# Experts with a bitwise threshold search and down products last, the last norm over two stages, and filler products on TensorE ahead of four stages

## What is computed

```python
aff = jax.nn.sigmoid(flat_x @ gate_w + expert_bias)
_, topk_idx = jax.lax.top_k(aff, TOP_K)
mask = (topk_idx[:, :, None] == jnp.arange(E_r)[None, None, :]).any(axis=1)
score = jnp.where(mask, aff, -1.0).T
_, sel_idx = jax.lax.top_k(score, capacity)          # capacity = 1024 // 7 = 146
kept = jnp.take_along_axis(mask.T, sel_idx, axis=1)
w = jnp.where(kept, jnp.take_along_axis(aff.T, sel_idx, axis=1), 0.0)
out = jax.vmap(_ffn)(flat_x[sel_idx], routed_w1, routed_w2)
routed_sum = jnp.zeros_like(flat_x).at[sel_idx].add(out * w[:, :, None])
return shared_sum + routed_sum                       # x = x + gb * this
```

## Time and profile before

| what | value |
|---|---|
| median of three runs | 858.86 us (857.44 to 860.13) |
| profiled execution | 859.08 us |
| its span | 857.3 us |
| mean granted TensorE clock | 0.934 of full |
| busy PE, PEld, DVE, ACT, POOL | 727.9, 630.3, 615.7, 478.8, 376.4 us |
| norm ahead of the experts | 740.0 to 754.5 us |
| experts | 754.5 to 857.3 us |

### The profile page before, as it was taken

How to read it: one execution, slowest core, us unless ns; L and a number is a source line. 1 busy time by engine, 2 the same in 40 slices (tenths; PEclk the granted TensorE clock), 3 DMA queues, 4 the chain that set the end, 5 groups by cost and what they waited for, 6 DMA issues and landing times. The chain is left out here.

```text
span 857.3 us, 13269 instructions
## 1 busy us (share of the span) xinstructions
PE 727.9 (85%) x4368; PEld 630.3 (74%) x4368; DVE 615.7 (72%) x1313; ACT 478.8 (56%) x961; POOL 376.4 (44%) x389
## 2 busy tenths in 40 slices
PE   4769999899998999999999589972889998579980
PEld 2558888788887888878888489972667786548870
DVE  3645776667666776766776798986488878569988
ACT  2445666656675666755665434324587867155761
POOL 1193565515655156550451250002445544037883
PEclk9778999999999999999999989985899999889995
DMA  7340000000000000000000000004000000000001
GB/s 269 108 120 7 13 26 13 14 1 14 25 15 13 0 13 12 13 13 1 7 7 7 1 1 2 1 1 148 1 1 0 1 1 1 1 1 2 1 0 50
DMA packets 19723, 19.77 MB, mean 23 GB/s; under 512 B 1998, under 2 KB 17870, under 8 KB 19662
## 3 DMA queue, kind: packets, MB, share of 16 engines
q1 hardware_dynamic: 18334, 17.84, 6.6%
q10 hardware_dynamic: 1328, 1.18, 0.5%
HBM read 17.97 MB, written 1.05 MB: 22 GB/s over the span
## 5 line engine op out<-in xcount | busy, mean ns | idle before, releaser
L1000 POOL TENSOR_TENSOR at_swapped<-at_swapped,at_sin 128x512 f32<-128x512 f32 x40 | 51.7, 1292 | 180.0 <-ACT at_swapped L781 180.0
L816 ACT ACTIVATE at_probs<-at_probs,at_negmax 128x128 f32<-128x128 f32 (+7 forms) x128 | 99.5, 778 | 27.7 <-DVE at_negmax L895 24.5
L895 DVE CUSTOM_DVE_ANT_0 at_probs<-at_scores,causal 128x128 f32<-128x128 f32 (+7 forms) x128 | 96.4, 753 | 24.1 <-PE at_scores L698 21.9
L709 PE MATMUL at_turn<-ident_sb,at_probs 128*128 128x128 f32 x576 | 86.7, 278 | 12.2 <-DVE at_full_T_lo L910 11.4
L709 PEld LDWEIGHTS at_turn<-ident_sb,at_probs 128*128 128x128 f32 x576 | 67.6, 142 | 20.6 <-issue 6.5
L808 ACT ACTIVATE at_edge_T_hi<-at_turn 128x128 fp32r<-128x128 f32 (+3 forms) x128 | 55.5, 434 | 41.4 <-PE at_turn L709 41.1
L696 PE MATMUL at_scores<-at_kT_hi,room 128*128 128x512 f32 (+1 forms) x192 | 69.2, 360 | 10.6 <-POOL room L1022 5.1
L697 PE MATMUL at_scores<-at_kT_lo,room 128*128 128x512 f32 (+1 forms) x192 | 68.5, 357 | 0.0
L698 PE MATMUL at_scores<-at_kT_hi,room 128*128 128x512 f32 (+1 forms) x192 | 68.2, 355 | 0.0
L808 ACT ACTIVATE at_full_T_hi<-at_turn 128x512 fp32r<-128x512 f32 x64 | 38.3, 599 | 50.1 <-PE at_turn L709 48.3
L910 DVE TENSOR_TENSOR at_edge_T_lo<-at_turn,at_edge_T_hi 128x128 fp32r<-128x128 f32 (+3 forms) x128 | 61.3, 479 | 2.4 <-ACT at_edge_T_hi L808 2.4
(11 more groups left out here) (360 smaller groups left out, 2467.3 us busy)
## 6 DMA issues: line engine op xcount, KB each, us to landing
at_wq_in<-L_attn_Wqkv SPq DMA_DIRECT2D x16, 128.0 KB, 2.2
at_wo_in<-L_attn_Wo SPq DMA_DIRECT2D x16, 128.0 KB, 2.1
staging<-L_ffn_routed_w SPq DMA_DIRECT2D x7, 256.0 KB, 4.2
wmod<-L_wmod SPq DMA_DIRECT2D x3, 512.0 KB, 8.1
wmod<-L_wmod SPq DMA_DIRECT2D x1, 1536.0 KB, 11.4
x<-L_attn_x ACTq DMA_DIRECT2D x1, 1024.0 KB, 6.2
at_wkv_in<-L_attn_Wqkv SPq DMA_DIRECT2D x8, 128.0 KB, 4.7
staging<-L_ffn_w_gate SPq DMA_DIRECT2D x1, 1024.0 KB, 5.3
```

Of the source, the lines that this page charges most:

```text
L709: mm = pe.transpose(p_turn[t % 2][:, b - b0, :], probs[:, s % 4, b * P:(b + 1) * P], m.ident[:, :])
L816: act.activation(row, row, ACT.Exp, scale=-1.0, bias=negmax[:, s % 4:s % 4 + 1], accum_out=rowsum[:, s // NT % 2, i:i + 1])\
L895: dve.tensor_tensor_reduce(out=probs[:, s % 4, 0:width], in0=p_scores[s % 2][:, 0:width], in1=m.causal[:, S - width:], scale=-1.0, scalar= ...
L1000: pool.tensor_tensor(swapped[:, b, :], swapped[:, b, :], sin[:, cols], ALU.mult).then_inc(rope_turned, 1)
```

## The change

`keep_warm` issues matmuls of 128x512 whose output nobody reads: 5 at the end of `opening`, 7 and 9 around the first two transposes of `ffn0`, 50 and 12 around those of `attention1`'s first block, 12 and 12 at the end of its second.

`transposed_rows` is gone. The norm of tiles 0 to 3 goes into the tail of `attention1` (normalised by ScalarE with scale and bias, `spread`), with the variances of tiles 4 to 7; the rest of tiles 4 to 7 goes into `ffn1`.

In `ffn1` the sixteen half-expert slots run first, up products only, and all eight down products behind them, with `fed` kept for every expert. VectorE multiplies straight from PSUM (x1 isn't copied any more). The ranking is replaced by a search for each expert's 146th largest score, bit by bit, three bits a round: VectorE forms eight candidate bounds with a bitwise or, compares all scores with them, TensorE counts by a product with ones (eight matmuls of 64 columns), VectorE keeps the largest bound that at least 146 scores reach; ten rounds, in slots 4 to 13. Ties at the bound are ordered by a product in slot 14 (`find_order`, `weigh`). So the weights are there before the first down product, `y` is gone, and each output is added from PSUM; a bank's next product waits for its readers. GpSimd and ScalarE take tiles 0 and 1 in place of 6 and 7. The semaphores of the norms become shared ones; `steps`, a table of digits, is loaded by SP at `ffn1`'s start.

```diff
...
+def keep_warm(pe, out, w, count):
+    for _ in range(count):
+        pe.matmul(out, w[:, 0:P], w[:, 0:BANK], start=True, stop=True)
...
                 mod_columns(1, 0, 12)
+                keep_warm(pe, p_rows[0][:, :], wmod[:, 0, 0, :], 5)
...
+                idle_bank = p_gate[:, 0:2, :].rearrange("p e t -> p (e t)")
+                keep_warm(pe, idle_bank, m.room, 7)
                 turn_x(0)
                 turn_x(1)
+                keep_warm(pe, idle_bank, m.room, 9)
...
+                    keep_warm(pe, idle_bank[:, :], m.room, 50)
...
+                    keep_warm(pe, idle_bank[:, :], m.room, 12)
...
                     out_job(1, j)
+                keep_warm(pe, p_scores[1][:, BANK:S], m.room, 12)
...
+                keep_warm(pe, p_scores[1][:, BANK:S], m.room, 12)
...
+                load_table(act, m, ACT.Sqrt, 0)
+                variance_roots(act, m, FIRST_TILES, 5)
+                act.wait_ge(spread_ready, 1)
+                for n in FIRST_TILES:
+                    act.activation(ln_xn[:, n, :], m.x[:, n, :], ACT.Identity, scale=m.rstd[:, n:n + 1], bias=m.nbias[:, n:n + 1]).then_inc(ln_normed, 1)
+                for k in range(KD):
+                    act.wait_ge(ln_turned, k + 1)
+                    act.activation(ln_h32[:, k, :], ln_banks[k], ACT.Identity, scale=m.modcol[:, 1, 8 + k:9 + k], bias=m.modcol[:, 1, 6 + k:7 + k])\
+                        .then_inc(ln_scaled, 1)
+                variance_roots(act, m, LAST_TILES, 6)
...
+                def final_stats(tiles):
+                    for n in tiles:
+                        dve.wait_ge(proj_free, len(jobs) + 4 + n // 2 + 1)
+                        chain.step(dve.bn_stats(m.stats[:, n, :], m.x[:, n, :]))
+                chain = m.chain.on(dve)
+                add_out(1, 0)
+                add_out(1, 1)
+                final_stats(FIRST_TILES)
+                add_out(1, 2)
+                variances(dve, m, chain, FIRST_TILES)
+                add_out(1, 3)
+                inverse_roots(dve, m, chain, FIRST_TILES, 5)
+                spread(dve, m, FIRST_TILES).then_inc(spread_ready, 1)
+                final_stats(LAST_TILES)
+                variances(dve, m, chain, LAST_TILES)
+                for k in range(KD):
+                    cols = slice(0, BANK)
+                    dve.wait_ge(ln_scaled, k + 1)
+                    chain.run(dve.tensor_copy(m.hT.hi[:, k, cols], ln_h32[:, k, :]))
+                    dve.tensor_tensor(m.hT.lo[:, k, cols], ln_h32[:, k, :], as_f32(m.hT.hi[:, k, cols]), ALU.subtract)
...
-    transposed_rows(nc, m, sems, sb, 1, 6, "ln3")
     E8 = NE + 1
+    DIGIT, ROUNDS = 8, 10
...
+        by_row, p_aff, p_marked, score, p_kept = (part(2, n * NT * E8) for n in range(5))
+        cut = p_y[2][:, 1, DM - E8:DM]
+        counts, order = part(3, 0), part(3, DM)
...
+        POOL_TILES, OWN_TILES = (0, 1), (2, 3, 4, 5, 6, 7)
+        NP, NO = len(POOL_TILES), len(OWN_TILES)
+        slots = [(0, 0), (1, 0), (0, 1), (1, 1)] + [(e, c) for e in range(2, E8) for c in range(2)]
+        GATED_SLOTS = (0, 1, 2)
+        FIRST_ROUND = 4
+        ORDER_SLOT = FIRST_ROUND + ROUNDS
...
+                def count(r):
+                    pe.wait_ge(compared, r + 1)
+                    out = counts[:, :, :].rearrange("p t e -> p (t e)")
+                    for t in range(NT):
+                        mm = pe.matmul(out, ones[:, :], above[:, t, :, :].rearrange("p j e -> p (j e)"), start=(t == 0), stop=(t == NT - 1))
+                    mm.then_inc(counted, 1)
+                def find_order():
+                    pe.wait_ge(split_done, 2)
+                    pe.matmul(order[:, :, :], earlier[:, :], equal[:, :, :], start=True, stop=False)
+                    for t in range(NT):
+                        pe.matmul(order[:, :, :], ones[:, :], more[:, t:t + 1, :].broadcast_to([P, NT, E8]), start=False, stop=False)
+                    for t in range(NT - 1):
+                        rest = NT - 1 - t
+                        mm = pe.matmul(order[:, t + 1:, :], ones[:, :], equal[:, t:t + 1, :].broadcast_to([P, rest, E8]), start=False, stop=(t == NT - 2))
+                    mm.then_inc(ordered, 1)
...
+                            own = [t for t in OWN_TILES if t // 2 <= j]
+                            pooled = [t for t in POOL_TILES if t // 2 <= j]
+                            if own:
+                                pe.wait_ge(routed_added, NO * (e - 2) + len(own))
+                            if len(pooled) > 2 * j:
+                                pe.wait_ge(scaled_done, NP * (e - 2) + len(pooled))
...
+                find_logits(0)
+                up(0)
+                turn_x()
+                up(1)
+                pe.wait_ge(hT_ready, KD)
+                find_logits(1)
+                up(2)
+                turn_logits()
+                up(3)
+                for n in range(FIRST_ROUND, len(slots)):
+                    up(n)
+                    if n < ORDER_SLOT:
+                        count(n - FIRST_ROUND)
+                    elif n == ORDER_SLOT:
+                        find_order()
+                for e in range(E8):
+                    down(e)
...
+                load_table(act, m, ACT.Silu, 2)
+                feed_hi(2)
+                for n in range(3, len(slots)):
...
+                def middle(n):
+                    dve.wait_ge(x2_read, n + 1)
+                    if n >= 2:
+                        dve.wait_ge(fed_lo, n - 1)
+                    gate = act2[:, n % 2, :]
+                    if n in GATED_SLOTS:
+                        chain.run(dve.tensor_tensor(gate, p_x2[n % 2][:, :], gate, ALU.mult))
+                    dve.tensor_tensor(mid[:, n % 2, :], p_x1[n % 2][:, :], gate, ALU.mult).then_inc(mid_done, 1)
...
+                def compare(r):
+                    as_int = mybir.dt.int32
+                    digits = steps[:, r, :].unsqueeze(2).broadcast_to([P, DIGIT, E8])
+                    chain.run(dve.tensor_tensor(bounds[:, :, :].bitcast(as_int), cut.bitcast(as_int).unsqueeze(1).broadcast_to([P, DIGIT, E8]),
+                                                 digits, ALU.bitwise_or))
+                    dve.tensor_tensor(above[:, :, :, :], score[:, :, :].unsqueeze(2).broadcast_to([P, NT, DIGIT, E8]),
+                                      bounds[:, :, :].unsqueeze(1).broadcast_to([P, NT, DIGIT, E8]), ALU.is_ge).then_inc(compared, 1)
+                def raise_cut(r):
+                    dve.wait_ge(counted, r + 1)
+                    chain.run(dve.scalar_tensor_tensor(out=reached[:, :, :], in0=counts[:, :, :], scalar=float(CAPACITY), in1=bounds[:, :, :],
+                                                        op0=ALU.is_ge, op1=ALU.mult))
+                    chain.run(dve.tensor_reduce(cut if r + 1 < ROUNDS else last_cut[:, :], reached[:, :, :].rearrange("p j e -> p e j"), AX.X, ALU.max))
...
+                inverse_roots(dve, m, chain, LAST_TILES, 6)
+                spread(dve, m, LAST_TILES).then_inc(spread_ready, 1)
+                split_lo(0)
+                split_lo(1)
                 dve.memset(aff[:], -1.0).then_inc(aff_cleared, 1)
...
+                chain.step(dve.memset(best2[:], -1.0))
+                dve.memset(ones[:], 1.0)
+                dve.tensor_scalar(earlier[:, :], m.causal[:, S - P:], 0.0, None, ALU.is_lt)
+                middle(0)
+                split_x()
+                middle(1)
+                middle(2)
+                mark_best()
                 chain.settle()
...
+                dve.wait_ge(steps_in, 16)
+                compare(0)
+                middle(3)
+                for n in range(FIRST_ROUND, len(slots)):
+                    r = n - FIRST_ROUND
+                    if r < ROUNDS:
+                        raise_cut(r)
+                        if r + 1 < ROUNDS:
+                            compare(r + 1)
+                        else:
+                            split_ties()
+                    elif n == ORDER_SLOT:
+                        weigh()
+                    middle(n)
+                for j in range(PAIRS):
+                    dve.wait_ge(down_mm, j + 1)
+                    rows = m.x[:, 2 * j:2 * j + 2, :]
+                    dve.tensor_tensor(rows, p_y[j][:, :, :], rows, ALU.add).then_inc(shared_added, 1)
...
+                    for i, t in enumerate(OWN_TILES):
                         returned(dve, e, t)
                         if e > 1:
...
+                            dve.wait_ge(routed_added, NO * (e - 2) + i + 1)
+                        dve.scalar_tensor_tensor(out=m.x[:, t, :], in0=p_y[t // 2][:, t % 2, :], scalar=row_weight[:, t, e - 1:e], in1=m.x[:, t, :],
...
```

More of the change, by code:

```diff
@@ L175, in row_stats, with variances @@
     chain.run(dve.tensor_tensor(m.rstd[:, :], m.rstd[:, :], m.tiny[:, 1, :], ALU.mult))
-def variances(dve, m, chain, tiles, sqrt_in):
+def variances(dve, m, chain, tiles):
     chain.settle()
@@ L1780, in ffn1 @@
-        scaled = x1[:, :, 0:DM]
```

(24 more changed lines are left out.)

460 lines of the change are left out of this document (198 added, 262 removed).

## The result

The changed kernel takes 825.5 us, the median of four runs (822.92 to 826.42); the kernel before takes 858.35 beside them. The ratio is 0.961 (0.9583 to 0.9637), 32.9 us less. The forecast was 835.3 with a range of 828 to 844: the sign was right, the time lies 2.5 us under the range. The profiled execution took 822.92 for a span of 821.1, 1.8 around it as before, but it is the fastest of the four; a second profile of the same kernel [e12] has a span of 823.5, near the middle of the runs.

The account below looks back on a forecast made before the run. Norm was taken as a VectorE chain; the experts as bound by TensorE, then by VectorE's late adds. Norm and experts 20.3, second attention 2.8, first feed-forward 0.5: 23.6 off 857.3, giving 835.3 us for the median, range 828 to 844.

Parts of the forecast that it names:

- the price of the ten counts: In the experts, TensorE's ten counts of eight 64-column matmuls: 0.85 us each, priced from transposes, 8.5 in all.
- The order: In the experts, TensorE's 16 small matmuls with a switch that order ties: 1.6 us.
- Rival A: In the experts, counts cost by their columns, 0.43 each, and the order 0.5: 5.3 us less, 830; chance 0.12.
- The norm: Ahead of the experts, splitting the norm over two stages lets the experts begin 5.8 us earlier.
- The adds: Beside the down products, VectorE's six PSUM adds per expert take 2.4 us under TensorE's 2.84, unstretched by GpSimd; nothing stalls.
- C: In the experts' rounds, GpSimd blocks VectorE's SBUF reads, 4.3 us per slot: +7 to 8, 843; chance 0.09.
- D: In the experts, all five VectorE ops of a slot are held, 7.5 us per slot: +38, 873; chance 0.03.
- B: The fillers miss and the clock is low at each restart, second attention, first feed-forward, experts: +6.7, 842; chance 0.12.
- The second attention: Fillers keep its transposes and eight projections warm: 1.3 and 1.5, together 2.8 us less.
- the narrow case: In the second attention, a 1.9 us gap behind 50 fillers keeps the high clock; if it falls, 0.5 is left.
- The first feed-forward: Warm transposes give ScalarE the first chunk 0.5 us earlier; the faster 24 gate products are worth nothing.
- The opening: Five fillers end over 2.2 us before the first attention, so the clock falls: worth 0; if it held, 1.2.

Follow-up runs that it names:

- e12: The changed kernel itself, unedited, timed and profiled once more: 825.28 us, ratio 0.9616 to the kernel before.
- e6: The changed kernel with the counts' comparison result and ones in float32 in place of bfloat16: 839.81 us, ratio 0.9792 to the kernel before.
- e5: The changed kernel with each count's eight matmuls of 64 columns issued twice: 826.98 us, ratio 0.9645 to the kernel before.
- e4: The changed kernel with the last norm back in one stage of its own, no fillers in the attention's tail: 830.72 us, ratio 0.9685.
- e7: The changed kernel with VectorE's 42 adds reading an SBUF tile in place of PSUM, leaving out routed outputs of six tiles: 828.27 us, ratio 0.965.
- e8: The changed kernel with each comparison of 512 elements done four times in a row: 836.78 us, ratio 0.9758 to the kernel before.
- e3: The changed kernel without any filler, waits and order kept: 829.13 us, ratio 0.9658 to the kernel before.
- e1: The changed kernel without the five fillers at the end of the opening: 824.31 us, ratio 0.9611 to the kernel before.
- e2: The kernel before with the five opening fillers and nothing else: 858.18 us, ratio 1.0011.
- e9: The kernel before with three more VectorE copies at the end of the opening, 1.0 us of work: 855.91 us, ratio 0.9975.
- e10: The kernel before with six more VectorE copies at the end of the opening, 2.0 us of work: 858.5 us, ratio 1.0007.
- e13: The changed kernel with four fillers in each of the first attention's four groups, ahead of the second value projection: 827.21 us, ratio 0.9627.
- e14: The kernel before with four fillers in each of the first attention's four groups and nothing else: 854.77 us, ratio 0.9962.

## Why the forecast was too high

**The sum by stages.** The forecast of 23.6 had 20.3 for norm and experts, 2.8 for the second attention, 0.5 ahead of it. Measured against the profile before: norm and experts 26.8 (6.4 and 20.4), second attention 2.7, and ahead of it 4.3 by e12, which has the median's span. These are 33.8, against 32.9 in the medians. So the miss has two parts: norm and experts brought 6.5 more than forecast, and what lies ahead of the second attention 3.8 more. Either one alone would have left the time inside the range (828.8 or 831.5); it took both.

**Experts: the terms.** The step that failed is the price of the ten counts, "8.5". Measured: 0.24 for the eight matmuls and 0.09 on the next product, 3.3 for ten, 5.2 less. The order took 0.54 for 1.6, from the same rows: 1.1 less. The product step is 0.2295 (2.754 for twelve) and not 0.235, which is 1.1 less over 192; the down products take 2.88 and not 2.84, 0.3 more. Waits in front of products add up to 1.2, not 1.75. Together 7.6 less; TensorE's part of the experts was 6.4 shorter than forecast, so about 1.2 was missing from the list. I put it down to breaks where one form follows another, which nothing here measures one by one. The end behind TensorE took 0.4 more than forecast. Rival A had nearly the right price for a count (0.43 against 0.33) and for the order (0.5 against 0.54), and too low a chance, 0.12. I held against it that 128-column steps never come under 0.10; these rows were float32, the counts are bfloat16, and e6 shows what type alone does to the same 64 columns: 0.03 us a matmul in one, 0.21 in the other. The Trainium skill's figure, weighed and set aside in the prediction, was the right one: "TensorE: Matmul & The Clock Gate", section "Back-to-back issue gap", has about 25 ns up to 64 columns, e5 has 29. The same page, section "LDWEIGHTS (loading the stationary operand)", puts a load of 128 columns at 128/1.2 = 107 ns, and its section "Weight-path perf modes — Fast Weight Load (FWL) and DoubleRow" gives the fast load only to operands that aren't FP32; e6's 106 ns per record agrees with the first, and e5 against e6 with the second.

**The norm.** Forecast 5.8, measured 6.4 in the stages; the whole kernel loses 5.2 in e4. The chain came out as added up: the second fillers and VectorE's last split end together. Right.

**The adds.** Right, and e7 shows why: from PSUM the adds stay 0.40 apart beside GpSimd; from SBUF each that meets one of GpSimd's takes twice as long. TensorE never waits for a bank.

**Rounds.** VectorE's part of a slot was 2.2 in the sum and is 2.14; C and D didn't come (e8: 0.95 of slack). B didn't either: behind the fillers of the second attention and ahead of the experts TensorE's products are at the high level.

**The second attention.** 2.8 against 2.7. The fillers took 13.2 us and not 11.8, since they themselves begin cold, so the gap behind them is 0.59 and not 1.9; the narrow case was never tried:

```profile
577.24 13.21 PE L66 MATMUL at_idle<-room 128*128 128x512 f32 x50 [1.88 <-PEq L1090]
591.04 1.97 PE L1399 MATMUL at_bank<-ident_sb,at_g_row 128*128 128x128 f32 x16 [0.59 <-DVE at_g_row L1429]
592.76 2.99 PE L66 MATMUL at_idle<-room 128*128 128x512 f32 x12
597.00 0.47 PE L57 MATMUL at_proj<-hT_hi,at_pT_lo 128*128 128x512 f32 x1 [1.25 <-PEq L1350]
```

**The first feed-forward.** Forecast 0.5; e3's profile has 94.60 without fillers and the changed kernel's 94.60 with them: 0. The stage isn't the same in every execution, though: with this code it takes 96.7 and 96.8 in the profiles of e1 and e7, where TensorE waits 4.15 us for VectorE ahead of the last down product and not 2.66. Its 24 gate products are warm and, as said, worth nothing.

**The opening.** Said to be 0 because the gap would be over 2.2. The gap is 0.30 and the head is warm, and the result is 0 nevertheless (e1, e2). The reason given was wrong, so the 0 was luck: where the clock held, the prediction said 1.2. Against the same products of the kernel before, the changed kernel has gained 1.2 at 38 us, 0.6 is left at 52, and 1.2 is there again at 58.6. That the median shows none of it is inside the spread between executions.

**Ahead of the second attention.** 3.8 of the miss lie here, in no term of the sum. The prediction compared with the span of one profile, in which three of four groups had a patch that the changed kernel's first profile lacks or has shorter. Across them the changed kernel's lead over the same products grows by 1.0, 1.5 and 1.4 us. It took the first attention as given. In the seventeen profiles of this study, one for each kernel and two of the changed one, the stretch from its first product to the end of the first feed-forward takes 538.7 to 546.4 us; the kernel before's profile is the longest. e9 moves the kernel before by more than 1 us of work costs, the other way. That the code alone doesn't decide whether a patch follows a gap is shown by the same group being cold in one profile of the same kernel and warm in another (the changed kernel and e12 above). Seven profiles have the changed kernel's code up to there, and they part by the time at which the first attention begins, which differs by 2 us between executions:

| profile | begins | first attention | patches past 75 us |
|---|---|---|---|
| changed, e6, e7 | 35.4 to 36.1 | 445.0 to 445.3 | none |
| e4, e5, e8 | 34.1 to 34.2 | 447.4 to 447.7 | at 261 |
| e12 | 34.7 | 448.1 | at 170 |

So those that begin later take less. This fits a patch that depends on when a gap falls, as do e9 and e10 for the kernel before; no run of the changed kernel sets that moment by itself. Why the changed kernel's executions have fewer of them in the middle stays open: neither its opening fillers (e1, e2) nor all its fillers account for it (without any, in e3, the first feed-forward ends at 578.8, against 581.8 before).

## What to carry to other kernels

Price a small matmul by rows of its own type: here 64 columns cost 29 ns in bfloat16 and twice 106 in float32, and a search by counting on TensorE is nearly free in the first. Adds that wait for a late weight are worth moving behind it and beside the products, read straight from PSUM, if the search that gives the weight fits into the slack of the products' slots. Before a change of a few us is priced from one profile, look whether its cold stretches are the same in a second profile of the same kernel. Fillers that closed one gap removed the patches there and left new ones elsewhere (e13, e14).

## What the runs showed of the hardware

The kernel before became 2.1 us faster by the ratio (0.7 to 3.7) with 1 us of work added (e9). A float32 filler of 512 columns is two records of 0.456 us; a float32r one is one of 0.23. Each of GpSimd's adds stretches one VectorE add of 256 columns with both inputs in SBUF from 0.47 to 0.91 us or more (e7, 14 of 42); with one input in PSUM none is stretched (0.40 apart, six in 2.44 us). Executions of the same code begin the first attention at 34.1 to 36.1 us, and those that begin at 35.4 or later take 2.2 to 3.1 us less for it than the others.
